# A 5x5 depthwise and grouped convolution in 64x64 quarter products over 6 shifts instead of full 128x128 products over 4

## The chip, the cores and the metric

The kernel runs on one core of a Trainium2 chip. The metric is the device time of one execution, in microseconds (us). The chip's engines work side by side and meet through semaphores: PE (TensorE) multiplies matrices, DVE (VectorE) and ACT (ScalarE) work on vectors and empty PE's accumulator memory (PSUM), POOL (GpSimd) works on vectors in SBUF, SP (SyncE) here only issues DMAs. "PEld" is the load of PE's weights.

## The reference

The input x has 8 images of 256 channels on 64x64 points, in float32. There are two layers, each with a group normalisation ahead of it and a sum with x behind it. Layer 1 is a block-sparse attention that the change does not touch. Layer 0, in its core:

```python
qkv = _conv2d(x, w_qkv)                                    # 256 -> 768 channels, 1x1
agg = _conv2d(qkv, w_dw, groups=3 * td, pad=SCALE // 2)    # 5x5, each channel by itself
agg = _conv2d(agg, w_pw, groups=3 * HEADS)                 # 8 channels -> 8 channels, 1x1
ms = jnp.concatenate([qkv, agg], axis=1)
...
q, k = relu(q), relu(k);  kv = sum over points of k v;  out = q kv / (q sum k)
x = x + _conv2d(out, w_proj)
```

The two convolutions behind qkv are what is changed. 768 channels are 96 groups of 8 channels ("heads" of one of q, k, v), and both convolutions together map the 8 channels of a head to 8 channels through 5x5 taps: tap times mix.

## The kernel before

Each image is worked on alone (the loop over `b`), and layer 0 does it in two passes `g` of 128 channels of each of q, k and v. A pass runs these stages in order:

1. `qkv`: 24 products of the normalised image with the weights (L686), emptied into three padded tiles `RAW[j]` (j for q, k, v) on 128 partitions.
2. sums of k v over the points for the raw half (`kv_sums(0)`, L643 to L655).
3. the convolution, `conv`: 24 pairs of heads.
4. sums for the convolved half (`kv_sums(1)`).
5. attention of the convolved half and the projection (`attend(1, c)`, `project`, L709 and L711), eight chunks of 512 points. In the second pass DVE also takes the statistics of the finished image for layer 1 there (`plane_stats`, L1217).

The 64x64 points are split into 16 planes (every fourth row by every fourth column), each 16x16 with a border of one, so 17x17 = 289 numbers are stored. A head of 8 channels and 16 planes fills the 128 partitions: SP loads it by a DMA from `RAW` into `IN` (L362), and a 5x5 convolution over the points is then four products of 128x128, one for each shift of 0 or 1 in the two directions (L623), over 256 columns. A pair of heads is 8 such products. The weights for them ("toeplitz") are built by POOL, tap times mix, in two operations of 128x512 a pair (L485), from taps that SP loads for eight heads at once (L350). The 2x256 results of a pair lie in one PSUM bank of 512 columns. They are emptied by ACT for even items and by DVE for odd ones (L930 to L932; the helper's lines are L982, L985, L1144 and L1147) into `OUTG`, and two DMAs store them to `AGG` (L374).

PSUM has four banks for this work, used in turn. Each user has an item number `i` and the bank `i % 4`. `claim(i)` on PE waits until the bank's last user has been emptied, `hand(i)` tells the engine that empties it. Before the change a pair is one item. From pair 11 on there is, after every second pair, an `attend(0, c)`: two items, one with the denominators (WD) and one with the numerators (WN), each a product of 512 columns (L666). ACT copies the denominators (L1030), DVE takes their reciprocal (L1234) and multiplies the numerators by it (L1238), which frees their bank. DVE does its share in the order of the program: it empties a pair's bank, then does the division, then the next pair's.

SP issues in program order too: the load for pair k, which waits until PE is through with pair k-3, then the store of pair k-2, which waits until it is emptied. Every DMA here has 128 rows.

X itself stays in natural order in SBUF. The planes are read out of it by strides: with 16 planes a row of 16 numbers has a step of 4 numbers. That is so where layer 0 normalises X into XN (`norm_chunk`, L1010 on ACT and L1207 on DVE), where the projection is added to X (L1247 on DVE, L491 on POOL) and where the statistics are read (L1217).

## Time and profile before

| | |
|---|---|
| median of 3 runs | 9082.88 us (9064.64 to 9105.43) |
| the profiled execution | 9057.69 us, span 9055.9 us |
| PE busy | 7636.7 us, 84% |
| DVE busy | 5037.9 us, 56% |
| POOL, ACT busy | 3786.7 us, 3520.5 us |
| DMA | 431.90 MB in 398743 packets |
| mean granted PE clock | 0.919 of full |
| chain that ended last | PE 54%, DVE 23%, issue 7%, DMA 6% |

A busy share is a mean over stages with different limits. PE is the busiest engine, and the chain that ended last is PE for a little over half of its length; L623, the convolution, is the largest line of it with 12%. In a group of matmuls the mean duration is longer than the pace, since they overlap. One float32 product shows as two matmul records and two weight loads.

### The profile page before, as it was taken

To read this page: it belongs to the slowest core of one execution; us is meant where nothing else is said; L and a number is where in the kernel's file an instruction comes from. 1 tells how busy PE (TensorE), PEld (TensorE's weight loads), DVE (VectorE), ACT (ScalarE), POOL (GpSimd) and SP (SyncE) were. 2 spreads that over 40 slices of the span, in tenths; PEclk is the share of its full clock that TensorE was granted. 3 is DMA by queue.
4 is the path that set the end of the run, shared out by engine and by line. 5 is a ranking of instruction groups with operands and counts; after the bars stand their busy time and mean duration, and the time that the engine had idled before them with its cause. 6 is when DMAs were issued, how large, how long until landed. Compare 5 with 4: busy or idle time off the path is not lost.

```text
span 9055.9 us, 206227 instructions
## 1 busy us (share of the span) xinstructions
PE 7636.7 (84%) x65004; PEld 5190.5 (57%) x65004; DVE 5037.9 (56%) x11563; ACT 3520.5 (39%) x9207; POOL 3786.7 (42%) x10084
## 2 busy tenths in 40 slices
PE   8978799787997879978899778997789977799788
PEld 5655556555565555655555555565555555566555
DVE  3475644756447564475644756447564475644655
ACT  1145621445214552145521455215552155511555
POOL 2345533445334553345533444334443344533444
PEclk9988999888999889988999888998889988999888
DMA  3201122011220112201122111221112211122111
GB/s 101 65 16 26 41 87 65 16 26 38 89 65 16 27 42 85 65 18 26 51 75 65 21 22 49 77 65 21 23 53 73 65 22 22 57 68 65 24 20 55
DMA packets 398743, 431.90 MB, mean 48 GB/s; under 512 B 159184, under 2 KB 355984, under 8 KB 393296
## 3 DMA queue, kind: packets, MB, share of 16 engines
q1 hardware_dynamic: 397648, 418.42, 16.3%
q8 instruction: 550, 9.01, 0.4%
q14 instruction: 545, 4.46, 0.2%
HBM read 102.76 MB, written 67.63 MB: 19 GB/s over the span
## 4 chain that ended last, share of the span: by engine, by line
PE 54%; DVE 23%; issue 7%; DMA 6%; ACT 5%; DVEq 3%; SPq 1%; POOL 0%; ACTq 0%; POOLq 0%
PE PS L623 12%; PE PS L686 7%; DVE arena L1144 5%; PE PS L913 5%; DVE arena L1234 4%; PE PS L778 3%; PE PS L666 3%; PE PS L878 3%; PE PS L838 3%; PE PS L847 3%; DVE SM L1379 3%; ACT arena L1088 3%; DVEq L1367 2%; DMA kv_rows<-arena 2%; PE PS L654 2%
## 5 line engine op out<-in xcount | busy, mean ns | idle before, releaser
L982 ACT ACTIVATE arena<-PS 128x128 f32<-128x128 f32 (+5 forms) x4160 | 1552.0, 399 | 1947.5 <-PE PS L623 596.5
L561 POOL COPY arena<-arena 64x129 f32 x6144 | 1527.9, 291 | 1372.0 <-PE PS L884 1094.0
L485 POOL TENSOR_TENSOR arena<-arena 128x512 f32<-128x512 f32 x768 | 806.2, 1072 | 1459.5 <-PE PS L623 1443.6
L623 PE MATMUL PS<-arena 128*128 128x256 f32 x6144 | 1359.1, 379 | 46.4 <-DMA arena<-arena 46.3
L1144 DVE COPY arena<-PS 64x260 f32<-64x260 f32 (+2 forms) x1272 | 634.3, 515 | 1352.5 <-PE PS L623 524.7
L623 PEld LDWEIGHTS PS<-arena 128*128 128x128 f32 x6144 | 1155.4, 189 | 270.6 <-issue 98.0
L1144 DVE COPY arena<-arena 64x129 f32 x4096 | 840.9, 267 | 398.3 <-PE PS L884 285.9
L1234 DVE RECIPROCAL arena<-arena 128x512 f32<-128x512 f32 x256 | 857.5, 3350 | 119.1 <-ACT arena L1030 117.5
L818 PE MATMUL PS<-arena 64*64 64x192 f32 x8192 | 699.0, 386 | 256.9 <-POOL arena L561 242.0
L491 POOL TENSOR_TENSOR BUF<-BUF,arena 128x512 f32<-128x512 f32 x256 | 358.2, 1399 | 1282.3 <-ACT arena L1018 1282.3
L1379 DVE TENSOR_REDUCE SM<-PS 128x1 f32<-128x384 f32 x1024 | 570.6, 558 | 539.7 <-issue 434.3
L1088 ACT ACTIVATE arena<-PS,SM 128x384 f32<-128x384 f32 x1024 | 595.1, 581 | 638.9 <-DVE SM L1379 598.6
L778 PE MATMUL PS<-W,BUF 128*128 128x192 f32 x4096 | 818.7, 348 | 27.2 <-ACT BUF L1010 20.5
L778 PEld LDWEIGHTS PS<-W,BUF 128*128 128x128 f32 x4096 | 687.2, 197 | 63.2 <-ACT BUF L1010 21.2
L686 PE MATMUL PS<-BUF,W 128*128 128x512 f32 x1536 | 678.8, 604 | 37.5 <-DVE BUF L1207 33.7
L825 PE MATMUL PS<-CST,arena 128*128 128x128 f32 x1024 | 312.1, 337 | 415.9 <-ACT arena L1088 379.7
L838 PE MATMUL PS<-CST,arena 128*128 128x128 f32 x3072 | 589.2, 307 | 52.0 <-ACT arena L1088 51.2
L878 PE MATMUL PS<-arena 128*64 128x65 f32 x12288 | 632.8, 243 | 0.0
L538 POOL TENSOR_TENSOR arena<-arena,SM 128x256 f32<-128x256 f32 x512 | 314.4, 614 | 748.1 <-DVE SM L1322 746.7
L878 PEld LDWEIGHTS PS<-arena 128*64 128x64 f32 x12288 | 483.9, 149 | 196.1 <-issue 193.9
L1147 DVE TENSOR_SCALAR arena<-PS 128x256 f32<-128x256 f32 (+1 forms) x336 | 160.1, 477 | 733.0 <-PE PS L623 432.7
L666 PE MATMUL PS<-arena 128*128 128x512 f32 x1024 | 498.4, 608 | 68.8 <-DVE arena L1241 56.0
(102 smaller groups left out, 10563.4 us busy)
## 6 DMA issues: line engine op xcount, KB each, us to landing
arena<-arena SPq DMA_DIRECT2D x1024, 128.0 KB, 2.3
arena<-arena SPq DMA_DIRECT2D x768, 144.5 KB
BUF<-in_x SPq DMA_DIRECT2D x18, 2048.0 KB, 12.0
kv_rows<-arena SPq DMA_DIRECT2D x256, 130.0 KB, 3.5
arena<-kv_rows SPq DMA_DIRECT2D x256, 130.0 KB
out<-BUF SPq DMA_DIRECT2D x64, 512.0 KB, 2.6
arena<-in_taps SPq DMA_DIRECT2D x96, 288.0 KB, 3.6
W<-in_w SPq DMA_DIRECT2D x2, 768.0 KB, 5.8
```

The costliest lines, as they stand in the source:

```text
L485: last = pool.tensor_tensor(o, tap, mix, ALU.mult)
L561: last = pool.tensor_copy(G[p % GD][0:D, j // 3, j % 3, :], KVB[0:D, bass.ds(off, KVW)])
L623: last = nc.tensor.matmul(bank(i)[:, a * 256:(a + 1) * 256], lhsT=TW[n % 2][:, a * CH + k * P:a * CH + (k + 1) * P], rhs=src[:, k // 2:k / ...
L686: last = nc.tensor.matmul(bank(i), lhsT=W0[:, kt, (2 * j + g) * P:(2 * j + g + 1) * P], rhs=XN[:, kt, c * CH:(c + 1) * CH], start=(kt == 0 ...
L778: last = nc.tensor.matmul(PS[:, p % 2, u * 3 * D:(u + 1) * 3 * D], lhsT=XN[:, kt, t * P:(t + 1) * P], rhs=W1[:, kt, h, :], start=(kt == 0) ...
L838: last = nc.tensor.transpose(PS[:, 4 + p % 2, i * P:(i + 1) * P], PR[p % 2][:, i * P:(i + 1) * P], ident)
L878: nc.tensor.matmul(PS[D * blk:D * (blk + 1), 6 + t % 2, at:at + D1], lhsT=PT[p % 2][:, i * P + D * blk:i * P + D * (blk + 1)], rhs=G[p % G ...
L982: return nc.scalar.activation(o, i, ACT.Copy)
L1088: nc.scalar.activation(PR[p % 2].rearrange("p (i s c) -> p s i c", i=3, s=2), PS[:, 2 * (p % 2):2 * (p % 2) + 2, 0:3 * D].rearrange("p s ( ...
L1144: return nc.vector.tensor_copy(o, i)
L1234: order.after(nc.vector.reciprocal(DN[c % 2], DN[c % 2]))
L1379: nc.vector.tensor_reduce(NM[:, p % 2:p % 2 + 1], PS[:, 2 * (p % 2):2 * (p % 2) + 2, 0:3 * D], AX.XY, ALU.max, negate=True).then_inc(s_nm, 1)
```

## The change

Two by two positions replace the four by four in one direction: the points are now split into 8 planes (every fourth row by every second column), each 16x32 with a border, stored as 17x34 = 578. A head of 8 channels and 8 planes fills 64 partitions, and a pair of heads 128. So a pair is loaded by one DMA from 16 channels that lie on every fourth partition, and stored by one. A 5x5 convolution is now six shifts (two in rows, three in columns) of 64x64 weights. Each product covers 8 rows of 32 points, 256 columns; the two heads and the two halves of the rows make four quarter products for a shift, 24 for a pair. Head `a` sits on partitions 64a to 64a+63 of the input and writes bank `i + a`; half `o` of the rows goes to partitions 64o to 64o+63 of the output. A pair is now two items: ACT empties head 0, DVE head 1, each in two operations of 64x256.

```diff
-PL, R = 16, 16
-PW = R + 1
-PAD = PW * PW
+PL, R, RC2 = 8, 16, 32
+PW, PC = R + 1, RC2 + 2
+PAD = PW * PC
+SHIFTS = 6
-    return g * HALF_ITEMS + (I_CQ + m + 8 if m < 0 else I_CKV + m + 2 * max(0, (m - 2) // 2))
+    return g * HALF_ITEMS + (I_CQ + 2 * (m + 8) if m < 0 else I_CKV + 2 * m + 2 * max(0, (m - 2) // 2))
...
         def natural(tile, fy):
-            return tile.rearrange("p (r fy c fx) -> p fy fx r c", fy=4, c=R, fx=4)[:, fy]
+            return tile.rearrange("p (r fy c fx) -> p fy fx r c", fy=4, c=RC2, fx=2)[:, fy]
...
                         if n >= 3:
                             wait_filled(sp, b, conv_item(n - 3))
+                            settle(sp)
+                            wait_filled(sp, b, conv_item(n - 3) + 1)
...
-                        for a in range(2):
-                            sp.dma_start(IN[n % 3][:, a * PAD:(a + 1) * PAD],
-                                         head_rows(RAW[j], 2 * pr + a).rearrange("p (f n) -> p f n", f=PL)
-                                         ).then_inc(s_in[n % 3], 16)
+                        sp.dma_start(IN[n % 3], pair_rows(RAW[j], pr).rearrange("p (f n) -> p f n", f=PL)
+                                     ).then_inc(s_in[n % 3], 16)
...
-                        for k in range(24 + 2):
+                        for k in range(24 + 3):
                             if k < 24:
                                 load_pair(24 * g + k)
-                            if k >= 2:
-                                store_pair(24 * g + k - 2)
+                            if k >= 3:
+                                store_pair(24 * g + k - 3)
...
-                        for a in range(2):
...
-                            tap = tap.unsqueeze(2).broadcast_to([P, 4, 8, 16])
-                            mix = dw[:, hh, 64:72].unsqueeze(1).unsqueeze(3).broadcast_to([P, 4, 8, 16])
-                            last = pool.tensor_tensor(o, tap, mix, ALU.mult)
-                        last.then_inc(s_tw, 1)
+                        tap = tap.unsqueeze(2).broadcast_to([P, SHIFTS, 8, 8])
+                        mix = dw[:, 8 * SHIFTS:].unsqueeze(1).unsqueeze(3).broadcast_to([P, SHIFTS, 8, 8])
+                        pool.tensor_tensor(o, tap, mix, ALU.mult).then_inc(s_tw, 1)
...
                                 claim(i)
+                                claim(i + 1)
...
-                                for a in range(2):
-                                    src = IN[n % 3][:, a * PAD:(a + 1) * PAD].rearrange("p (r c) -> p r c", r=PW)
-                                    for k in range(4):
+                                for k in range(SHIFTS):
+                                    for a, o in ((0, 0), (1, 1), (0, 1), (1, 0)):
+                                        head = slice(a * D, (a + 1) * D)
+                                        rows = IN[n % 3][head, :].rearrange("p (r c) -> p r c", r=PW)
+                                        y, xx = k // 3 + o * R // 2, k % 3
                                         last = nc.tensor.matmul(
-                                            bank(i)[:, a * 256:(a + 1) * 256],
-                                            lhsT=TW[n % 2][:, a * CH + k * P:a * CH + (k + 1) * P],
-                                            rhs=src[:, k // 2:k // 2 + R, k % 2:k % 2 + R],
-                                            start=(k == 0), stop=(k == 3))
-                                hand(i, last)
+                                            bank(i + a)[o * D:(o + 1) * D, 0:256],
+                                            lhsT=TW[n % 2][head, k * D:(k + 1) * D],
+                                            rhs=rows[:, y:y + R // 2, xx:xx + RC2],
+                                            start=(k == 0), stop=(k == SHIFTS - 1))
+                                        if k == SHIFTS - 1 and o != a:
+                                            hand(i + a, last)
...
-                    if i % 2 == e:
-                        wait_filled(eng, b, i)
-                        eng.wait_ge(s_og[n % 3], b * 512 + 32 * (n // 3 + 1))
-                        op(OUTG[n % 3], PS[:, i % 4, :]).then_inc(s_free[e], 1)
+                    i = conv_item(n) + e
+                    wait_filled(eng, b, i)
+                    eng.wait_ge(s_og[n % 3], b * 256 + 16 * (n // 3 + 1))
+                    op(OUTG[n % 3][e * D:(e + 1) * D, 0:256], PS[0:D, i % 4, 0:256])
+                    op(OUTG[n % 3][e * D:(e + 1) * D, 256:512], PS[D:P, i % 4, 0:256]).then_inc(s_free[e], 1)
```

The taps that the host lays out follow the same split; a load of them is 128x224 numbers instead of 128x576.

Three places show how the change moves the instructions. First PE, at the first of a pass's eight attends and the two pairs behind it: L666 (now L669) is the attend, L623 (now L625) the convolution. Before:

```order
L666 MATMUL PS<-arena 128x512 [waits bank_freed_by_act]
L666 MATMUL PS<-arena 128x512 [waits bank_freed_by_dve]
L605 REGISTER_ALU
L618 REGISTER_ALU [waits bank_freed_by_act]
L619 REGISTER_ALU [waits toeplitz_built]
L623 MATMUL PS<-arena 128x256 [waits conv_in0]
L623 MATMUL PS<-arena 128x256 x7
L618 REGISTER_ALU [waits bank_freed_by_dve]
L623 MATMUL PS<-arena 128x256 [waits conv_in1,toeplitz_built]
L623 MATMUL PS<-arena 128x256 x7
```

And now:

```order
L669 MATMUL PS<-arena 128x512 [waits bank_freed_by_act]
L669 MATMUL PS<-arena 128x512 [waits bank_freed_by_dve]
L603 REGISTER_ALU
L617 REGISTER_ALU [waits bank_freed_by_dve,bank_freed_by_act]
L618 REGISTER_ALU [waits toeplitz_built]
L625 MATMUL PS<-arena 64x256 [waits conv_in0]
L625 MATMUL PS<-arena 64x256 x23
L603 REGISTER_ALU
L617 REGISTER_ALU [waits bank_freed_by_dve,bank_freed_by_act]
L625 MATMUL PS<-arena 64x256 [waits toeplitz_built,conv_in1]
```

A pair waits for two banks, one from each engine, and is 24 products instead of 8. The attend's numerators lie in the bank that the second pair behind it claims.

Next DVE, some rows on in the same stage: the multiplication by the reciprocal, and what follows until the next reciprocal. Before:

```order
L1238 TENSOR_TENSOR arena<-PS,arena 128x2x16x16 [waits item_for_dve,dve_order]
L318 REGISTER_ALU
L931 REGISTER_ALU [waits item_for_dve]
L1144 COPY arena<-PS 128x512 [waits conv_out1]
L1233 REGISTER_ALU
L1234 RECIPROCAL arena<-arena 128x512 [waits bank_freed_by_act]
```

And now:

```order
L1241 TENSOR_TENSOR arena<-PS,arena 128x16x32 [waits item_for_dve]
L317 REGISTER_ALU
L933 REGISTER_ALU [waits item_for_dve]
L1147 COPY arena<-PS 64x256 [waits conv_out0]
L1147 COPY arena<-PS 64x256
L1147 COPY arena<-PS 64x256 [waits conv_out1,item_for_dve]
L1147 COPY arena<-PS 64x256
L1236 REGISTER_ALU
L1237 RECIPROCAL arena<-arena 128x512 [waits bank_freed_by_act]
```

DVE empties half of both pairs between two divisions, where it emptied the whole of one.

Last SP, the loads (L362) and stores (L374) of two pairs. Before:

```order
L362 DMA arena<-arena 128x1x289 [waits item_for_dve]
L362 DMA arena<-arena 128x1x289
L372 REGISTER_ALU
L374 DMA arena<-arena 8x16x256 [waits bank_freed_by_act]
L374 DMA arena<-arena 8x16x256
L318 REGISTER_ALU
L362 DMA arena<-arena 128x1x289 [waits item_for_act]
L362 DMA arena<-arena 128x1x289
```

And now:

```order
L362 DMA arena<-arena 128x1x578 [waits item_for_act,item_for_dve]
L371 REGISTER_ALU
L374 DMA arena<-arena 16x8x512 [waits bank_freed_by_act,bank_freed_by_dve]
L362 DMA arena<-arena 128x1x578 [waits item_for_act,item_for_dve]
L371 REGISTER_ALU
L374 DMA arena<-arena 16x8x512 [waits bank_freed_by_act,bank_freed_by_dve]
```

Four DMAs a pair became two, with twice the bytes each, and the store is that of the pair whose completion the load ahead of it has waited for.

## Rows read from the trace of the kernel before

**Rows 1.** Timeline of PE: the first twelve pairs of one pass, and one attend

```profile
1218.12 14.10 PE L623 MATMUL PS<-arena 128*128 128x256 f32 x64
1233.33 14.07 PE L623 MATMUL PS<-arena 128*128 128x256 f32 x64 [1.11 <-DMA arena<-arena]
1248.29 10.61 PE L623 MATMUL PS<-arena 128*128 128x256 f32 x48 [0.89 <-DMA arena<-arena]
...
1262.62 1.88 PE L666 MATMUL PS<-arena 128*128 128x512 f32 x4
```

**Rows 2.** Timeline of PE: two pairs between attends, and the pass's last pairs

```profile
1297.16 1.88 PE L666 MATMUL PS<-arena 128*128 128x512 f32 x4
1298.88 7.08 PE L623 MATMUL PS<-arena 128*128 128x256 f32 x32
1305.79 1.88 PE L666 MATMUL PS<-arena 128*128 128x512 f32 x4
...
1320.34 0.32 PE L654 MATMUL PS<-CST,arena 128*128 128x128 f32 x1 [2.31 <-DMA arena<-arena]
```

**Rows 3.** Groups by line and shape: busy us, mean ns | idle before, releaser

```profile
L485 POOL TENSOR_TENSOR arena<-arena 128x512 f32<-128x512 f32 x768 | 806.2, 1072 | 1459.5 <-PE PS L623 1443.6 <-DMA arena<-in_taps 15.8
L1144 DVE COPY arena<-PS 64x260 f32<-64x260 f32 x512 | 198.8, 428 | 57.7 <-PE PS L762 50.6
L982 ACT ACTIVATE arena<-PS 64x256 f32<-64x256 f32 x528 | 196.6, 372 | 74.0 <-PE PS L762 65.3 <-PE PS L723 8.6
L1247 DVE TENSOR_TENSOR BUF<-PS,BUF 128x512 f32<-128x512 f32 x128 | 138.9, 1085 | 34.7 <-PE PS L711 34.7
L1217 DVE BATCH_NORM_STATS2 SM<-BUF 128x6 f32<-128x512 f32 x128 | 130.0, 1067 | 0.0
L1241 DVE TENSOR_TENSOR arena<-PS,arena 128x512 f32<-128x512 f32 x128 | 88.5, 692 | 7.2
L1160 DVE BATCH_NORM_STATS2 SM<-BUF 128x6 f32<-128x512 f32 x144 | 88.4, 679 | 2.3 <-DMA BUF<-in_x 2.3
```

**Rows 4.** Source line L818, 64x64 products, one set: ns min/median/max, first and last start

```profile
L818 PE MATMUL PS<-arena x8: 321/334/374, 2915.0 to 2915.2; 64*64 64x192 f32 x8
```

**Rows 5.** Timeline of PE: the same set

```profile
2915.01 0.56 PE L818 MATMUL PS<-arena 64*64 64x192 f32 x8
```

**Rows 6.** Timeline of DVE and of ACT behind the attend at 1297.16

```profile
1298.85 3.35 DVE L1234 RECIPROCAL arena<-arena 128x512 f32<-128x512 f32 x1 [0.71 <-ACT arena L1030]
1302.23 0.69 DVE L1238 TENSOR_TENSOR arena<-PS,arena 128x512 f32<-128x512 f32 x1
...
1298.22 0.60 ACT L1030 ACTIVATE arena<-PS 128x512 f32<-128x512 f32 x1 [3.64 <-PE PS L666]
```

**Rows 7.** Timeline of SP's queue, ahead of the pair at 1248.29

```profile
1243.36 1.37 SPq L362 DMA_DIRECT2D arena<-arena  x2
1244.85 1.35 SPq L374 DMA_DIRECT2D arena<-arena  x2
```

**Rows 8.** Busy us by stretch: PE PEld DVE ACT POOL, PEclk, DMA share, GB/s

```profile
1218.10:1262.60 44.50, 42.32 (x204) 36.17 (x193) 4.10 (x8) 3.59 (x6) 25.68 (x24) 1.00 0.47 146
2885.00:2915.00 30.00, 23.25 (x355) 15.41 (x353) 21.15 (x74) 21.68 (x63) 18.80 (x76) 1.00 0.07 16
1320.30:1331.30 11.00, 9.04 (x125) 6.55 (x126) 6.02 (x8) 2.49 (x8) 0.00 (x0) 0.54 0.01 1
```

**Rows 9.** Timeline of DVE: the end of layer 0 in the second pass

```profile
494.92 0.69 DVE L1241 TENSOR_TENSOR arena<-PS,arena 128x512 f32<-128x512 f32 x1
...
502.40 5.85 DVE L1217 BATCH_NORM_STATS2 SM<-BUF 128x6 f32<-128x512 f32 x6
```

**Rows 10.** Timeline of DVE: L1207 as an image begins, and in layer 1

```profile
1154.28 7.00 DVE L1207 TENSOR_SCALAR BUF<-BUF,SM 128x1024 f32<-128x1024 f32 x4
...
512.00 2.98 DVE L1207 TENSOR_SCALAR BUF<-BUF,SM 128x1024 f32<-128x1024 f32 x4
```

79 lines of the change are left out of this document (40 added, 39 removed).

## The prediction, made before the changed kernel ran

> **What bounds the kernel now.** I read the page first: PE is busy 84% of the span and is 54% of the chain that ended last, so an engine's share alone doesn't say what a stage waits for. The timeline of PE over one convolution does. In its first half PE runs pair after pair without a gap but for two waits of 1.11 and 0.89 us on the load of a pair [rows 1]. 64 passes take 14.10 us there, the last of them 0.38 us long by its record, so the pace is (14.10 - 0.38) / 63 = 0.218 us for 256 columns, and a pair of 16 passes takes 3.46 us. In the second half, pairs and attends follow without any gap: an attend every 1305.79 - 1297.16 = 8.63 us, made of 1.72 for the attend and 6.91 for two pairs [rows 2]. Both halves are bound by PE, and its clock is full in them [rows 8]. The timelines of DVE and ACT say what lies beside it: behind an attend that starts at 1297.16, ACT copies the denominators from 1298.22, DVE's reciprocal runs 3.35 us from 1298.85, and its multiplication ends at 1302.92 [rows 6]. That is 5.76 us after the attend's start, and today nobody waits for it. At the end of the second pass it is DVE that has no gap: from 494.92 to 508.25 it works without a pause, and layer 1 waits for it [rows 9].
>
> **PE's part.** A pair was 8 products, 16 passes; now it is 24 quarter products, 48 passes of 256 columns. What they cost depends on how many quarters run at once, and L818 shows such products: the same four positions in the same order, heads on the halves of the rows, banks apart. A set of eight passes over 192 columns takes 0.56 us, and one pass by itself is recorded with 0.321 [rows 4, 5]. 192 columns at the pace above are 0.163 us, which leaves 0.158 of latency. One after another the set would take 8 x 0.163 + 0.158 = 1.46 us, two at a time 0.81, four at a time 0.48. It takes 0.56, so four run together, with 0.08 for the start. In a long row of such passes the start is paid once, and a round of four costs the columns of one, 0.218 us. 12 rounds: 2.61 us a pair, against 3.46. The weights of 64 columns are loaded beside that, as those of L623 are today. The bounds: 2.61 from below; from above, if each round costs half a set, 0.28 + 0.055 for the 64 more columns, 12 x 0.335 = 4.0 us. I take 2.61, since rows 4 and 5 are one set and its second round starts within 0.24 us of the first.
>
> *First half, twelve pairs.* Today 1262.62 - 1218.12 = 44.5 us [rows 1]. Then 12 x 2.61 = 31.3, if the waits on loads go too. They should: SP spends 1.37 + 1.35 us a pair on issuing four DMAs [rows 7], and with two it spends about 1.4. The load of a pair now waits for nothing but PE's end with the pair three back, so it has two pairs, 5.2 us, to land. The load issued from 1243.36 let PE start at 1248.29, 4.9 us later, with a second issue of 0.68 in between [rows 1, 7]; 4.2 are left. Gain: 13.2 us a pass, and there are 16 passes: 211 us.
>
> *Second half, six cycles from attend to attend.* Here the faster PE meets a wait. The second pair behind an attend claims the bank of its numerators, which DVE frees 5.76 us after the attend began. PE is there after 1.72 + 2.61 = 4.33. So the cycle is 5.76 + about 0.1 for the semaphore + 2.61 = 8.47 us, and against 8.63 only 0.16 x 6 x 16 = 15 us are gained; the other 1.5 us a cycle are idle. DVE's emptying of the first pair comes behind the multiplication and is late for nobody: the next attend claims that bank 2.6 us later. The tail behind pair 23 ends with DVE's divisions and a wait on the stores (2.31 us, [rows 2]), both as now: 0, at most 1 us a pass.
>
> **Emptying.** ACT and DVE each do two operations of 64x256 a pair, by like rows 0.37 and 0.43 us each [rows 3], so up to 0.9 us a pair on each. In the first half 2.61 us a pair cover it; in the second the two sums (0.9 behind the multiplication, 0.9 ahead of the copy of the denominators, where 1.06 are free) stay under cover too. If that cover went, each 0.1 us would cost 0.1 x 96. POOL's weights go from 2 x 1.07 us to one operation of 384 elements, between 0.8 and 1.07 us, hidden either way: 0.
>
> **DMA.** The bytes stay, the packets double in size and halve in number. The engines are busy 0.47 of the first half [rows 8]; by bytes that becomes 0.47 x 3.7 / 2.61 = 0.67, by packets 0.33. I take no wait from it.
>
> **The strides.** Where planes are read out of X the step goes from four numbers to two. That is in no name of the change, but it is in the chain. Over 512 numbers L1247 takes 1085 ns and L1217 1067, with a step of four; L1241 and L1160, the same kinds of operation without a step, take 692 and 679 [rows 3]. A step of two is in no row. It may cost the whole 0.39 us still, or nothing. A price that goes by steps would be near the middle, one that goes by how many numbers lie close together near nothing. I take nothing, since the one measured excess (0.39 of 0.69) is less than a doubling, and two neighbours would share it. The Trainium skill (SBUF — State Buffer, "Door 1: The DMA port swizzle") says that SBUF is read in lines of 16 bytes and that two hits on a line are enough for full speed. By that, four numbers' step has one hit a line and pays, two has two and is free; the sum would be the same as mine, and no run here shows it yet. In the second pass DVE does 8 of L1247 and 16 of L1217 in one unbroken row [rows 9]: 24 x 0.38 = 9.1 us an image, a few tenths less where PE is the limit in the first chunks; 8 x 8.8 = 70 us. In the first pass PE sets the pace there: 0. As an image begins, PE waits for the first of four L1207, which take 7.00 us instead of layer 1's 2.98 [rows 10]; a quarter of the difference, 1.0 us, 8 times: 8 us.
>
> **Sum.** 211 + 15 + 70 + 8 = 304 us off 9057.69: 8754 for an execution like the profiled one. That one is 25 us under the median of the runs shown, which gives a predicted median of 8778 us.
>
> **Rivals.**
> - *The strides give nothing.* For it: no row has a step of two. Against it: the thought above. The time: 8778 + 78 = 8856. Chance 0.17.
> - *The rounds don't chain.* Each shift's four quarters wait for the four before, for weights or for the sums in PSUM, and a pair costs between 3.0 and 4.0 us. For it: rows 4 and 5 show two rounds, not twelve. At 3.4: the first half gains 44.5 - 40.8 = 3.7 x 16 = 59, the cycle is 5.86 + 3.4 = 9.26 and loses 0.63 x 96 = 60, the strides stay: 9005. At 4.0 it is 9178, slower. Chance 0.09. The Trainium skill (TensorE: Matmul & The Clock Gate, "Part 3: Packing small matmuls — row/col tiling") gives 3.07 for four tiles where the ideal is four; on this kernel's 48 passes of 0.218 that would be 3.41 us a pair, near this case's 3.4, and the trace has 0.56 for a set where one after another would be 1.46.
> - *Only two quarters run at once*, in two halves of the array. A pair is 24 x 0.218 = 5.23 us: the first half 62.8, 18.3 more; the cycle 1.72 + 10.46 = 12.2, 3.55 more, six times; 16 x (18.3 + 21.3) = 634 more, minus 78: 9639 us, slower. It decides from 3.6 us a pair on, where gain and loss meet. Against it: the set's 0.56 is under the 0.81 of two at a time. Chance 0.05.
> - *A wait takes PE's place in the first half*: loads that land later at 0.67 of the DMA engines, so that a pair takes 3.1 us and not 2.61. It costs 0.49 x 12 x 16 = 94 us: 8872; where the later loads reach the second half too, 8915. Chance 0.06.
> - *The clock falls in the new gaps.* PE idles 1.5 us of every 8.5. In the attention of layer 1, where PE is busy 23.25 of 30 us, the clock stayed full; behind the wait of 2.31 us it fell, and the stretch from 1320.3 on had 0.54 [rows 8]. Each cycle in which the second pair runs at 1.2 GHz costs 2.61 us; a third of them 84 us: 8862. Chance 0.04.
>
> **Chances and range.** The forecast has 0.59. The range: down to 8690, if the tail and the emptying give something back and the start of an image gains more; up to 8910, which takes in the strides, the waits and the clock. What can be told from no change is 0.5%, 45 us. Faster: 0.59 + 0.17 + 0.06 + 0.04 and half of the unchained case, 0.91. Within 0.5%: 0.02. Slower: 0.07.
>
> **What would show it.** In the profile of the changed kernel: passes of L625 with a busy time of 2.6 us a pair; twelve pairs in 31 to 32 us without a wait on a DMA; attends 8.4 to 8.5 us apart with an idle time of 1.5 us that DVE's multiplication ends; the operations on X at 0.69 us instead of 1.08; SP's queue with 1.4 us a pair. I am wrong if a pair's passes take over 3 us, if the attends move apart, or if L1217's successor still takes over 0.9 us.

## The result, and the profile after

The changed kernel took 8942.72 us (median of 4 runs, 8914.77 to 8950.0) against 9076.4 us before in the same session (4 runs): a ratio of 0.984, 95% interval 0.981 to 0.9875. It is faster by 134 us where 304 were forecast, and the median lies above the upper end of the range, 8910 us.

The profiled execution of after has a span of 8935.5 us, 120 us less than before. The starts of the same instructions in the two traces split it up (all 8 images, 16 passes; "first half" from the first pair of a pass to its first attend, "second half" the six cycles from attend to attend):

| part | forecast | measured |
|---|---|---|
| first half, 45.04 to 35.02 us a pass | -211 | -160 |
| second half, 52.02 to 54.60 us a pass | -15 | +41 |
| tail of the convolution, two kinds of pass | 0 | +6 |
| second pass, attention to statistics, 57.77 to 51.39 us | -70 | -51 |
| start of an image, 16.49 to 15.75 us | -8 | -6 |
| layer 1, 640.7 to 646.6 us an image | 0 | +47 |
| sum | -304 | -123 (spans: -120) |

The 3 us between the two sums are in stages that the change does not touch. The 6 us at the start of an image are within scatter: seven such starts last from 13.4 to 18.3 us in after, and in the second trace of the same kernel their mean is 16.4. Now the views. Pairs are counted from 0. First PE's timeline over the same pass as [rows 1] (start, us, engine, line, operation, count, and in brackets the idle time ahead and what ended it):

```profile
1208.10 10.59 PE L625 MATMUL PS<-arena 64*64 64x256 f32 x192
1218.86 2.82 PE L625 MATMUL PS<-arena 64*64 64x256 f32 x48 [0.17 <-issue]
1222.77 8.00 PE L625 MATMUL PS<-arena 64*64 64x256 f32 x144 [1.08 <-issue]
1231.65 5.72 PE L625 MATMUL PS<-arena 64*64 64x256 f32 x96 [0.88 <-issue]
1237.67 5.56 PE L625 MATMUL PS<-arena 64*64 64x256 f32 x96 [0.30 <-issue]
1243.16 1.99 PE L669 MATMUL PS<-arena 128*128 128x512 f32 x4
1245.08 2.82 PE L625 MATMUL PS<-arena 64*64 64x256 f32 x48
1249.47 2.82 PE L625 MATMUL PS<-arena 64*64 64x256 f32 x48 [1.57 <-DVE arena L1241]
1252.23 1.99 PE L669 MATMUL PS<-arena 128*128 128x512 f32 x4
```

Four pairs in a row, 192 passes, take 10.59 us, one pair by itself 2.82; so three pairs add 7.77, 2.59 us each. That is the forecast's 2.61: the rounds of four chain. But the first half has four breaks, where the kernel before had the two of [rows 1] and one of 0.19 us, and between two attends there is a wait on DVE's L1241. Attends are 1252.23 - 1243.16 = 9.07 us apart, where [rows 2] had 8.63. The page calls the breaks "issue". In the trace every one of the 77 breaks over 0.15 us in the 16 first halves ends 0.09 to 0.14 us behind the last landing of the load for the pair that then starts, and together they make 3.5 us a pass. They are not all at pairs 4 and 8: most of the time goes at pairs 6 (0.9 us a pass in the mean), 4 (0.7) and 8 (0.5), and the other pairs from 5 on have 0.2 to 0.4 each.

SP's queue over the first breaks (L362 load, L374 store, L349 the taps), and POOL's building of the weights of pair 3:

```profile
1211.02 0.54 SPq L362 DMA_DIRECT2D arena<-arena  x1
1211.99 0.56 SPq L374 DMA_DIRECT2D arena<-arena  x1
1214.57 0.33 SPq L349 DMA_DIRECT2D arena<-in_taps  x1
1215.09 0.54 SPq L362 DMA_DIRECT2D arena<-arena  x1
1215.81 0.57 SPq L374 DMA_DIRECT2D arena<-arena  x1
1216.50 0.69 SPq L362 DMA_DIRECT2D arena<-arena  x1
...
1213.69 0.85 POOL L484 TENSOR_TENSOR arena<-arena 128x384 f32<-128x384 f32 x1 [1.74 <-PE PS L625]
```

An issue costs 0.55 us at the least and 0.68 in the mean of the first halves, 1.4 us a pair for the 2.7 of [rows 7]. The load of pair 4 could have gone when PE was through with pair 1, at 1213.51. It went at 1215.09, behind the taps, which waited until POOL had built the weights of pair 3, at 1214.54. Four transfers then leave within 2.6 us, and the load issued at 1216.50 lands at 1222.68, 6.2 us later; PE starts its pair at 1222.77.

DVE and ACT around the attend at 1243.16:

```profile
1243.32 0.86 DVE L1147 COPY arena<-PS 64x256 f32<-64x256 f32 x2 [1.88 <-PE PS L625]
1244.96 3.35 DVE L1237 RECIPROCAL arena<-arena 128x512 f32<-128x512 f32 x1 [0.78 <-ACT arena L1033]
1248.44 0.69 DVE L1241 TENSOR_TENSOR arena<-PS,arena 128x512 f32<-128x512 f32 x1
...
1244.33 0.60 ACT L1033 ACTIVATE arena<-PS 128x512 f32<-128x512 f32 x1 [0.28 <-PE PS L669]
```

The chain is that of [rows 6], each link a little later: the denominators 1.17 us behind the attend's start (1.06), the division 1.80 (1.69), the multiplication's end 5.97 (5.76). Then 0.34 us to the pair's start (forecast 0.1) and 2.76 from there to the next attend (forecast 2.61).

The windows of this pass's two halves (length, busy us of PE, PEld, DVE, ACT and POOL, clock, DMA share, GB/s), against [rows 8]:

```profile
1208.10:1243.20 35.10, 32.58 (x577) 25.14 (x577) 9.89 (x25) 8.35 (x22) 12.31 (x13) 1.00 0.79 172
1243.20:1297.80 54.60, 44.89 (x603) 26.61 (x600) 34.45 (x36) 12.70 (x30) 18.11 (x17) 1.00 0.52 127
```

The clock stays full through the gaps. The DMA engines' share rose from 0.47 to 0.79, not to 0.67 (0.79 is also its mean over all 16 first halves). And the groups that answer to [rows 3] (busy us, mean ns, idle before):

```profile
L625 PE MATMUL PS<-arena 64*64 64x256 f32 x18432 | 1063.4, 378 | 196.3 <-DVE arena L1241 154.5 <-issue 25.2 <-DMA arena<-arena 14.3
L1250 DVE TENSOR_TENSOR BUF<-PS,BUF 128x512 f32<-128x512 f32 x128 | 87.7, 685 | 59.0 <-PE PS L714 57.9
L1220 DVE BATCH_NORM_STATS2 SM<-BUF 128x6 f32<-128x512 f32 x128 | 81.0, 679 | 0.0
L484 POOL TENSOR_TENSOR arena<-arena 128x384 f32<-128x384 f32 x384 | 331.8, 866 | 1782.9 <-PE PS L625 1775.7
```

L1250 and L1220 are the old L1247 and L1217: 685 and 679 ns for 1085 and 1067. L1241's 154.5 us of idle time in front of L625 are 1.6 us in each of 96 cycles.

### The profile page after: what moved, and what is told of

It reads as the page before. It is cut to its first block, busy times and chain, and to the rows that moved or that the text cites. A ratio compares the mean times of both kernels' runs of the same rounds, so it can differ in the third digit from the quotient of the medians.

```text
span 8935.5 us, 233739 instructions
## 1 busy us (share of the span) xinstructions
PE 7402.7 (83%) x77292; PEld 4819.9 (54%) x77292; DVE 5140.2 (58%) x12139; ACT 3664.1 (41%) x9783; POOL 3287.1 (37%) x9700
## 4 chain that ended last, share of the span: by engine, by line
PE 51%; DVE 26%; issue 8%; ACT 6%; DMA 5%; DVEq 3%; POOL 1%; SPq 0%; POOLq 0%; ACTq 0%
PE PS L625 8%; PE PS L689 8%; DVE arena L1237 8%; DVE arena L1147 5%; PE PS L916 5%; PE PS L781 3%; PE PS L881 3%; PE PS L841 3%; PE PS L850 3%; DVE SM L1382 3%; DMA kv_rows<-arena 3%; PE PS L669 3%; ACT arena L1091 2%; DVEq L1370 2%; PE PS L657 2%
## 5 line engine op out<-in xcount | busy, mean ns | idle before, releaser
L985 ACT ACTIVATE arena<-PS 128x128 f32<-128x128 f32 (+4 forms) x4544 | 1667.7, 390 | 2185.4 <-PE PS L625 782.5
L1147 DVE COPY arena<-PS 64x256 f32<-64x256 f32 (+5 forms) x1656 | 762.8, 473 | 1209.9 <-PE PS L689 528.0
L625 PE MATMUL PS<-arena 64*64 64x256 f32 x18432 | 1063.4, 378 | 196.3 <-DVE arena L1241 154.5
L625 PEld LDWEIGHTS PS<-arena 64*64 64x64 f32 x18432 | 767.1, 133 | 516.4 <-issue 348.6
L484 POOL TENSOR_TENSOR arena<-arena 128x384 f32<-128x384 f32 x384 | 331.8, 866 | 1782.9 <-PE PS L625 1775.7
L821 PE MATMUL PS<-arena 64*64 64x192 f32 x8192 | 720.7, 393 | 244.7 <-POOL arena L559 227.2
L489 POOL TENSOR_TENSOR BUF<-BUF,arena 128x512 f32<-128x512 f32 x256 | 327.1, 1278 | 1296.7 <-ACT arena L1021 1296.7
L689 PE MATMUL PS<-BUF,W 128*128 128x512 f32 x1536 | 678.5, 604 | 31.3 <-DVE BUF L1210 23.0
L828 PE MATMUL PS<-CST,arena 128*128 128x128 f32 x1024 | 321.5, 347 | 433.2 <-ACT arena L1091 399.0
L841 PE MATMUL PS<-CST,arena 128*128 128x128 f32 x3072 | 605.3, 313 | 55.8 <-ACT arena L1091 54.8
L985 ACT ACTIVATE arena<-arena 64x129 f32 x2048 | 519.8, 300 | 93.5 <-POOL arena L522 48.8
L1150 DVE TENSOR_SCALAR arena<-PS 64x256 f32<-64x256 f32 (+1 forms) x528 | 224.2, 425 | 574.0 <-PE PS L658 303.5
```

Of the source, the lines that this page charges most:

```text
L625: last = nc.tensor.matmul(bank(i + a)[o * D:(o + 1) * D, 0:256], lhsT=TW[n % 2][head, k * D:(k + 1) * D], rhs=rows[:, y:y + R // 2, xx:xx ...
L689: last = nc.tensor.matmul(bank(i), lhsT=W0[:, kt, (2 * j + g) * P:(2 * j + g + 1) * P], rhs=XN[:, kt, c * CH:(c + 1) * CH], start=(kt == 0 ...
L821: last = nc.tensor.matmul(PS[D * blk:D * (blk + 1), 2 * (p % 2) + side, 0:3 * D], lhsT=(lower, upper)[side][:, cols], rhs=G[p % GD][rows, ...
L841: last = nc.tensor.transpose(PS[:, 4 + p % 2, i * P:(i + 1) * P], PR[p % 2][:, i * P:(i + 1) * P], ident)
L985: return nc.scalar.activation(o, i, ACT.Copy)
L1147: return nc.vector.tensor_copy(o, i)
```

## The experiments

All ratios are to the kernel before, timed in the same job; the intervals are of 95%. The theory at the start: the second half is set by DVE's hold on the numerators' bank; the first half by the loads; the operations on X run at the pace that was forecast for a step of two.

**The kernel after, once more** (no edit), the yardstick of its job.

> The changed kernel once more, beside the experiments of the same chip. Layer 1, which no edit touches, took 47 us more in its first profile than in that of the kernel before (32 attention stretches of 91 to 102 us, in both). If that is the phase of the clock and not the change, its 8 stretches from one statistics operation to the next come out anywhere within some 30 us of the 5126 of before, on either side, and the ratio to before stays at 0.98. If the change does slow layer 1, they stay at 5170 or more in this run and in all the others.

8936.34 us, ratio 0.9862 (0.9822 to 0.9902). First half 34.90, cycle 9.10, layer 1 646.2 us an image: each part comes back as it was.

**Four input buffers.** `IN` and its semaphores from three to four:

```
-        IN = [l0.take(PAD) for _ in range(3)]
+        IN = [l0.take(PAD) for _ in range(4)]
...
-                        if n >= 3:
-                            wait_filled(sp, b, conv_item(n - 3))
+                        if n >= 4:
+                            wait_filled(sp, b, conv_item(n - 4))
...
```

> Four input buffers instead of three, so a load starts a pair earlier. Theory A: in the first half of the convolution PE waits because a load now lands 5.5 us after its issue, later than the 5.2 us that two pairs take; then the twelve pairs go from 35.0 us (mean of 16 passes, start of the first to the first attend) to 31.5 to 32, and the kernel gets 50 us faster than the changed one (some 8890). Rival B: the DMA engines themselves are the limit (busy 0.79 there), so an earlier issue only makes each load take longer: the twelve pairs stay at 34 or more, gain under 15 us. Rival C: it is the weights of POOL or the emptying: no change at all.

8928.52 us, 0.9846 (0.9805 to 0.9887); first half 35.07, unchanged. The loads may start a pair earlier, but in the trace those of pairs 4 to 11 leave only 0.43 us earlier in the mean: they still stand behind the taps and the stores in SP's queue. And they take 0.48 us longer to land (5.90 for 5.42). A deeper buffer alone buys nothing.

**Numerators in banks of their own.** The raw half's numerators go to two PSUM banks outside the four, and the second pair behind an attend no longer waits for DVE's multiplication (its `claim` is changed to the bank's user before that, in lines that are not shown):

```
...
-                                hand(i, nc.tensor.matmul(bank(i), lhsT=w, rhs=q, start=True, stop=True))
+                                o = PS[:, (4, 7)[c % 2], :] if src == 0 and w is WN[0] else bank(i)
+                                hand(i, nc.tensor.matmul(o, lhsT=w, rhs=q, start=True, stop=True))
```

> The numerators of the raw half's attends go to the two PSUM banks that layer 0 leaves idle then, and the second pair behind an attend no longer waits for DVE's division. Theory A: the cycle from attend to attend (9.06 us now, 8.63 before the change) is set by that wait; it falls to what PE needs, 1.92 + 2.6 + 2.6 = 7.1 to 7.3 us, 16 x 6 x 1.8 = 175 us less: near 8770. Rival B: with the wait gone the loads are late here too, as in the first half: 7.8 to 8.3 us a cycle, 70 to 120 us less. Rival C: DVE itself is the limit, with 3.35 + 0.69 + 4 x 0.43 and its gaps, 6.0 us: then nothing below 7.1 can be seen and A holds.

8752.03 us, 0.9654 (0.9618 to 0.9689). PE's timeline:

```profile
1222.51 1.98 PE L675 MATMUL PS<-arena 128*128 128x512 f32 x4
1224.43 5.41 PE L630 MATMUL PS<-arena 64*64 64x256 f32 x96
1229.77 1.99 PE L675 MATMUL PS<-arena 128*128 128x512 f32 x4
```

No gap is left, the cycle from attend to attend is 7.26 us, and in the six cycles PE is busy throughout:

```profile
1222.51:1266.07 43.56, 43.56 (x605) 24.99 (x601) 34.45 (x36) 12.72 (x30) 18.15 (x17) 1.00 0.62 153
```

(9.10 - 7.26) x 96 = 177 us was the price of that wait. The cycle is made of 1.92 from attend to pair, 5.34 from there to the next attend: two pairs at 2.59 would be 5.18, and an attend took 1.72 between full products [rows 2]. So each cycle pays 0.2 us behind the attend and 0.16 ahead of it, where TensorE goes from whole-array products to quarters and back. The Trainium skill (TensorEngine Tiling (Array Packing), "Key Properties") says that a change of the tiling mode drains the engine. The trace fits that, with 0.36 us for two changes; no run here tells a drain from another cause.

**Without the division.** DVE's reciprocal of the raw half over one column instead of 512, so this run leaves out that division:

```
-                            order.after(nc.vector.reciprocal(DN[c % 2], DN[c % 2]))
+                            width = 1 if src == 0 else CH
+                            dn = DN[c % 2][:, 0:width]
+                            order.after(nc.vector.reciprocal(dn, dn))
```

> Leaves the reciprocal of the raw half's denominators out, but for one column. DVE frees the numerators' bank about 3.2 us earlier, 2.8 us behind the attend's start, before PE has ended the first pair at 4.5. Theory A: the same cycle as with other banks, 7.1 to 7.3 us, and beside it the end of a pass's raw attends gets shorter by the two divisions, 3 to 6 us a pass. So the kernel gains 175 + 50 to 100 us against the changed one: 8670 to 8720. Rival B (the wait isn't DVE's but that of the loads or of POOL): the cycle stays above 8 us.

8658.03 us, 0.9555 (0.9507 to 0.9602). The cycle is 7.26 again, the same by another road: bank or division, one link of one chain. The other 94 us against the banks are the tail of the convolution, from a pass's seventh attend to the convolved half's first: 20.1 us and not 26.0, since DVE's last divisions end the pass.

**The kernel before, once more** (no edit, one execution, so no ratio).

> The kernel before, unchanged, profiled once more. In the trace of before layer 1 of the eight images takes 5126 us (from the layer's statistics to the next ones), in the four traces of kernels with the change's layout 5169 to 5185. If that is an effect of the change (where its tensors lie or how the pace of the attention falls in), this trace has again 5120 to 5135; if the first profile was a lucky execution, 5150 to 5190. Layer 0's pieces are to come out as before: conv's first half 45.0 us a pass, six cycles of the second half 52.0 us.

9075.43 us. First half 45.26, cycle 8.65; layer 1 5142 us.

**Each load in two transfers of half the columns.**

```
+                        for a in range(2):
+                            part = slice(a * PAD // 2, (a + 1) * PAD // 2)
+                            sp.dma_start(IN[n % 3][:, part],
+                                         pair_rows(RAW[j], pr).rearrange("p (f n) -> p f n", f=PL)[:, :, part]
+                                         ).then_inc(s_in[n % 3], 16)
...
```

> The kernel after with each pair's load as two transfers of 289 columns, so packets of 1156 B instead of 2312 B; the same bytes and source partitions. Theory A, the size of the packets makes them slow (2312 B took 168 ns in the median, 1156 B 52 ns in the kernel before, so 1.6 times as much a byte): packets of 52 to 70 ns, landings 1 us earlier, the 3.2 us of waits on loads go from the 35.0 us of the first half (to 31.8 to 32.5), 16 passes: 40 to 50 us less than the kernel after, ratio to the kernel before 0.980. Rival B, the bytes in flight at once (loads and stores together at 172 GB/s) are the limit: packets take their share whatever their size, 75 to 85 ns for a half, first half 34.5 to 35.5, time within 10 us of the kernel after, 0.985. Rival C, SP's issues (two of 0.55 us and one of 0.56 us a pair, 1.7 of 2.6 us, and waits between them) become the limit: 3.1 us a pair, slower by 60 us, 0.992.

8921.25 us, 0.985 (0.9827 to 0.9873). The window of one first half:

```profile
1206.84:1241.34 34.50, 31.87 (x577) 25.68 (x577) 9.84 (x25) 8.37 (x22) 12.33 (x13) 1.00 0.63 169
```

The packets did get cheaper: 53 ns in the median for 1156 B (68 in the mean), where 2312 B had taken 168 (166), and the DMA share falls from 0.79 to 0.63 in this window, to 0.67 over all first halves. The first half's mean is 33.8 us, 1.2 less, between what theory A and rival B expected. The trace says why it isn't more. A load of pairs 4 to 11 has now landed 4.39 us behind its first issue, where it took 5.42. But it leaves 1.08 us behind the moment when its buffer is free, where it left after 0.65: SP issues three DMAs a pair and needs longer to catch up behind the taps. So the landing did get shorter by 1.0 us, and SP's queue took 0.4 of it back.

**Each load in two transfers of one head.** Packets of 2312 B as in after, each transfer to 64 partitions:

```
+                        for a in range(2):
+                            first = 64 * (pr // 4) + pr % 4 + 32 * a
+                            rows = RAW[j][first:first + 29:4, :].rearrange("p (f n) -> p f n", f=PL)
+                            sp.dma_start(IN[n % 3][a * D:(a + 1) * D, :], rows).then_inc(s_in[n % 3], 16)
...
```

> The kernel after with each pair's load as two transfers of one head each: packets stay 2312 B, each transfer reads 8 partitions instead of 16 and writes 64. It has the issues of the split by columns without its small packets. Theory A (size of the packets): packets stay at 150 to 170 ns, first half 35 us or a little more, time within 15 us of the kernel after. Rival B (limit by bytes): the same. Rival D, the many partitions that one transfer touches, or the queue that handles one transfer at a time, make it slow: two transfers in a row overlap less with one another, first half changes by over 1 us in either direction, time by over 15 us. With the split by columns faster and this one not, the size of the packets is shown.

8974.01 us, 0.9916 (0.9891 to 0.9941): slower than after, first half 37.2 us.

```profile
1221.44:1259.22 37.78, 33.09 (x576) 25.00 (x576) 9.80 (x24) 8.35 (x22) 12.29 (x13) 1.00 0.62 158
```

The share is again 0.62, but with less moved. With the same number of issues as the split by columns it is 3.4 us a pass worse. The packets of 2312 B take 122 ns in the median here (134 in the mean), not the 150 to 170 that theory A expected, so a packet's size alone doesn't set its time. Yet a pair's load needs 6.15 us from its first issue to its last landing. Which property of the transfer does that isn't shown. In the trace the semaphore of such a transfer is raised in 9 steps, that of a transfer to 128 partitions in 16, so fewer engines may share it. The Trainium skill (SBUF — State Buffer, "Door 1: The DMA port swizzle") has the 64 lower partitions reach only half of the ports; that would fit, but no view here shows ports.

**Banks, and loads and stores split.** The bank edit above, the split by columns, and the store split in the same way.

> The kernel after with three edits: the raw half's numerators in PSUM banks of their own (as in the banks experiment, 8752 us), each pair's load in two transfers of 1156 B packets and each pair's store in two of 1024 B packets. Theory A (size of the packets): the first half's waits go too, 3.2 us x 16 = 50 us less than 8752, so 8700, ratio 0.960. Rival B (limit by bytes): 8745 to 8760, 0.9655. Rival C (SP's four issues a pair, 2.2 us of 2.6): the pairs are paced by SP at 3 to 3.4 us, 8800 to 8850, 0.973.

8763.98 us, 0.9675 (0.9655 to 0.9695); first half 35.8 us, no better than after's 35.0. This doesn't refute that smaller packets help, since another limit took over. The loads have landed 3.88 us behind their first issue, sooner than in any other run, but they leave 2.43 us behind the moment when the buffer is free: SP's issues fill 27.7 us of the 35.8. That is rival C, the queue, though the time is less than the 8800 to 8850 it expected.

**The taps one pair later.** This changes the order of SP's queue:

```
-                        if n % 4 == 0 and 1 <= n // 4 <= 10:
+                        if n % 4 == 1 and 1 <= n // 4 <= 10:
```

> The kernel after with the load of the next taps issued ahead of the load of pairs 5, 9, 13, ... instead of 4, 8, 12, ... In the trace of the kernel after SP issued the taps at 1214.57, when GpSimd had built the weights of pair 3, and behind them within 2.5 us load 4, store 1 and load 5; load 4 could have gone at 1213.1, when pair 1 had freed its buffer. Theory E, the in-order queue: loads 4 and 8 go 1.5 us earlier and the transfers no longer come in a bunch, landings of loads 4, 5, 8 and 9 come before their pair, and the first half falls from 35.0 us to 32.5 to 33.5 a pass; 16 passes: 25 to 40 us less than the kernel after, ratio to the kernel before 0.982. Rival B, the transfers' volume is the limit: the wait only moves to other pairs, first half 34.5 to 35.2, time within 10 us of the kernel after. Rival F: the later taps are late for GpSimd's weights, pairs 5 and 9 wait on them, first half over 36, slower.

8910.92 us, 0.9827 (0.98 to 0.9855). PE's timeline of the pass:

```profile
1209.70 13.19 PE L625 MATMUL PS<-arena 64*64 64x256 f32 x240
1223.59 10.59 PE L625 MATMUL PS<-arena 64*64 64x256 f32 x192 [0.71 <-issue]
1234.46 2.82 PE L625 MATMUL PS<-arena 64*64 64x256 f32 x48 [0.27 <-DMA arena<-arena]
1237.70 5.44 PE L625 MATMUL PS<-arena 64*64 64x256 f32 x96 [0.42 <-issue]
```

SP's queue says why (the load of pair 4 is the third row):

```profile
1212.62 0.54 SPq L362 DMA_DIRECT2D arena<-arena  x1
1213.59 1.03 SPq L374 DMA_DIRECT2D arena<-arena  x1
1215.21 0.54 SPq L362 DMA_DIRECT2D arena<-arena  x1
1216.08 0.57 SPq L374 DMA_DIRECT2D arena<-arena  x1
1216.77 0.70 SPq L349 DMA_DIRECT2D arena<-in_taps  x1
1217.81 0.76 SPq L362 DMA_DIRECT2D arena<-arena  x1
```

Load 4 goes 5.5 us behind the pass's start, no longer 7.0, and pair 4 starts without a break. The waits that go there come back in part at pairs 5 and 9: the first half is 33.97 us, 1.05 less, and not the 1.5 to 2.5 expected. All loads now leave within 0.3 us of the moment when their buffer is free (in the mean of each pair), but they still take 5.58 us to land, and 2.5 us of breaks a pass remain. (The expectation's 1213.1 for pair 1's end is the start of its last product; the end is 1213.51.)

**Banks and later taps.** Both edits.

> The raw half's numerators in banks of their own (8752 us alone) and the taps' load one pair later. Theory E: the two are in different halves of a pass, so their gains add: 8752 less 25 to 40 is 8712 to 8727, ratio 0.962. Rival B: 8745 to 8760, 0.9655.

8743.82 us, 0.9645 (0.962 to 0.967). First half 34.44 against 34.62 with the banks alone: 3 us in 16 passes. Here the expectation of 25 to 40 us fails: by the first halves the later taps are worth 17 us in the kernel after and 3 us beside the banks, where the loads take 5.72 us to land. Why they land later there isn't shown.

**The same with four buffers for input and output.** The edits of four input buffers, and `OUTG` to four as well.

> As the last, and four buffers instead of three for the pairs' input and for their output. With the taps no longer ahead of load 4 the fourth buffer lets a load go 2.6 us earlier. Theory E with room left on the DMA engines: all waits on loads go, first half 31.5 to 32.3 us, time 8695 to 8710, ratio 0.960. Rival B, volume is the limit: landings take longer by what they start earlier, as in the run with four input buffers alone; time within 10 us of the run before this one.

8710.72 us, 0.9606 (0.9581 to 0.9631). PE's timeline:

```profile
1191.25 24.13 PE L630 MATMUL PS<-arena 64*64 64x256 f32 x432 [0.23 <-issue]
1216.51 8.00 PE L630 MATMUL PS<-arena 64*64 64x256 f32 x144 [1.13 <-issue]
```

First half 32.62 us. The fourth buffer, worth nothing while the taps stood in front of load 4, is now worth 1.8 us a pass: the loads leave 0.9 us earlier than without it, and take the same 5.7 us to land. The output's fourth buffer wasn't tried by itself, but the trace shows no part of it in the first half: a pair's emptying ends 0.94 to 1.04 us behind its last product with three as with four. So it is two things together: the queue must let the load go, and a buffer must be free for it.

**A step of four put back.** x is read by planes at a step of 4, in an order that is not the reference's:

```
-            return natural(X[:, kt, :], c // 2)[:, c % 2]
+            return X[:, kt, :].rearrange("p (r q c fx) -> p q fx r c", q=2, c=RC2, fx=4)[:, c // 4, c % 4]
```

> The kernel after with layer 0's x read and written by planes at a step of 4 fp32 in place of 2 (L1250's add, L1220's statistics and GpSimd's adds at L489), in an order that isn't the reference's, so this run leaves out which channel meets which; sizes and counts are as they were. It puts a step of 4 back where the change brought a step of 2. Theory A, the step sets their pace: the add of 512 columns takes 1085 ns again instead of 685, the statistics 1067 instead of 679, and the stretch from the second half's first raw chunk to the statistics 57.8 us instead of 51.4: 8 x 6.4 = 51 us more than the kernel after, 8987, ratio 0.9915. Rival: another part of the change (what stores or loads run beside them) made them faster: 685 and 679 ns stay and the time is that of the kernel after.

8983.08 us, 0.991 (0.9886 to 0.9934), and the groups:

```profile
L1250 DVE TENSOR_TENSOR BUF<-PS,BUF 128x512 f32<-128x512 f32 x128 | 138.7, 1083 | 34.9 <-PE PS L714 34.9
L1220 DVE BATCH_NORM_STATS2 SM<-BUF 128x6 f32<-128x512 f32 x128 | 130.0, 1070 | 0.0
```

The stretch is 58.0 us and the time 4 us from the expected 8987. The step sets the pace of these operations: nothing else was put back. The rule of the Trainium skill that was weighed ahead (SBUF — State Buffer, "Door 1: The DMA port swizzle", two hits on a line of 16 bytes) holds: the trace agrees, with 685 ns at two hits and 1083 at one.

**The order of the quarters.** The loops of a pair exchanged, the same 24 products:

```
-                                for k in range(SHIFTS):
-                                    for a, o in ((0, 0), (1, 1), (0, 1), (1, 0)):
+                                for a, o in ((0, 0), (1, 1), (0, 1), (1, 0)):
+                                    for k in range(SHIFTS):
```

> The kernel after with the two inner loops of a pair exchanged: all six shifts of one quarter in a row, then the next quarter, the same 24 products. Theory A, products overlap only with the neighbours in the program that are on other quarters: at most two quarters meet at the three borders, a pair takes 20 to 24 x 0.43 = 8.6 to 10.4 us instead of 2.6, 384 pairs: 2300 to 3000 us more, 11300 to 11900. Rival, TensorE looks ahead over several products and fills the quarters however they are ordered: 2.6 to 4 us a pair, under 9400.

10539.42 us, 1.1632 (1.1607 to 1.1656). The group of the quarter products:

```profile
L625 PE MATMUL PS<-arena 64*64 64x256 f32 x18432 | 2854.4, 379 | 1.7 <-issue 0.8
```

A pair takes 7.14 us for 2.59: 2854.4 us busy, not 1063.4. That is less than the 8.6 to 10.4 expected. The starts show why: in a row of one quarter five passes come 216 ns apart, while around a border they come in twos, 55 and 160 ns apart. So the overlap reaches some passes past the border, not one; but six shifts in a row are beyond it. The order of the loops is worth a factor of 2.75 on the same products.

**The kernel before without the division.** The edit of the run without the division, on the kernel before; this run leaves out the same division.

> The kernel before, with the raw half's reciprocal over one column instead of 512, so this run leaves out the division of the raw numerators. Theory A (in the kernel before TensorE's work of two pairs and an attend, 8.67 us, sets the second half's cycle, DVE has slack): the cycle stays at 8.6 to 8.7 us, and only the end of a pass, where DVE's divisions follow one another, is shorter by 6 us: 16 x 6 = 96 us less, 8960. Rival: DVE already set a part of the cycle and it falls under 8.5 us. On layer 1: if any shorter layer 0 costs it clock, layer 1 takes 5165 to 5190 us and the time is 8995; if it is the change itself, 5120 to 5150.

8992.6 us, 0.9925 (0.9904 to 0.9947). Its attends stay 8.645 us apart (8.670 in before):

```profile
1291.64 1.88 PE L666 MATMUL PS<-arena 128*128 128x512 f32 x4
1293.36 7.08 PE L623 MATMUL PS<-arena 128*128 128x256 f32 x32
1300.27 1.88 PE L666 MATMUL PS<-arena 128*128 128x512 f32 x4
```

In the old kernel the division was free in the cycle; in the new one it costs 1.84 us of each. Only the tail is shorter, by 5.0 us a pass.

**All edits, and loads split by columns.**

> As the run with banks, later taps and four buffers (8711 us), and each pair's load in two transfers of 289 columns (1156 B packets). Theory A (packets of 2312 B take 168 ns where two of 1156 B take 104): the 1.4 us a pass that is left of the waits on loads goes, 8680 to 8700. Rival (the queue of issues on SP, now three a pair, and the bytes are what is left): first half 32.6 us or more, 8705 to 8730.

8685.84 us (8684.5 to 8703.95), ratio 0.9589 (0.9567 to 0.9611), the fastest kernel that leaves nothing out. A pass's twelve pairs run as one row:

```profile
1182.60 31.59 PE L633 MATMUL PS<-arena 64*64 64x256 f32 x576 [0.23 <-issue]
```

First half 31.86 us in the mean, 0.76 less than without the split, 12 us in all. The medians differ by 25 us, but the intervals overlap, and in the two profiled executions layer 1, which no edit touches, differs by 17 us; so the other 13 us are not shown to be a gain.

## Why the prediction was wrong

The direction held, and so did the pair: 2.59 us measured, 2.61 forecast, and the order experiment shows what that rests on. The two rivals on the array, no chaining (3.4 us a pair) and two quarters at a time (5.23), are both far from it. The strides: a step of two is free, as taken (685 and 679 ns), shown by the step put back. Of their 78 us the last stage gave 51 and not 70, since some of DVE's saved time turns into waits on PE (L1247's idle time in [rows 3] was 34.7 us, its successor L1250 has 59.0); the 6 us at the start of an image are within scatter. The 8 forecast there were too many: they put the whole of 7.00 - 2.98 us down to the step. In the first image L1207 took 1.20 us at a step of four and its successor L1210 0.81 at a step of two, as in layer 1 without one; in the later images both have about 0.6 us more, whose cause isn't shown. SP's issue times came as forecast (1.4 us a pair). The emptying (376 and 423 ns) and POOL's weights (866 ns) stayed hidden.

**The step that failed in the first half** is "it has two pairs, 5.2 us, to land ... 4.2 are left", and with it "the load of a pair now waits for nothing but PE's end with the pair three back". The table has the loads of pairs 4 to 11 in the 16 first halves, from the starts and landings in the traces. "Leaves" is the first issue behind PE's end with the pair that frees the buffer when there are three of them, "lands" the last landing behind that first issue:

| run | leaves | lands | sum | first half |
|---|---|---|---|---|
| before (a pair 3.46 us) | 2.44 | 5.17 | 7.61 | 45.04 |
| by head | 0.81 | 6.15 | 6.96 | 37.22 |
| banks, loads and stores split | 2.43 | 3.88 | 6.31 | 35.79 |
| four input buffers | 0.22 | 5.90 | 6.12 | 35.07 |
| after | 0.65 | 5.42 | 6.07 | 35.02 |
| banks and later taps | 0.17 | 5.72 | 5.89 | 34.44 |
| later taps | 0.16 | 5.58 | 5.74 | 33.97 |
| split by columns | 1.08 | 4.39 | 5.47 | 33.80 |
| banks, later taps, four buffers | -0.71 | 5.70 | 4.99 | 32.62 |
| all these, and split by columns | -0.34 | 4.80 | 4.46 | 31.86 |

With quarter products the first half falls as the sum falls, from run to run; a mean under 5.2 still leaves single loads above it. The larger error is the landing: 5.42 us, not 4.2. The 4.2 came from one load of before with its second issue taken off; the mean of all of them there is 5.17, or 4.5 by the same reckoning. The smaller error is the 0.65 in SP's queue, 1.6 and 1.7 us for pairs 4 and 8 behind the taps, which wait for POOL, which waits for PE. Moving the taps took away nearly all of that and gave back 1.05 of the 3.5 us of breaks; the rest needed the fourth buffer and the split. A first half of 35.02 us for the forecast's 31.3 makes 60 us in 16 passes; the gain fell short by 51, since the sum started from one pass of 44.5 us where the mean before was 45.04.

The two breaks of [rows 1] lie four pairs apart, as the taps do, and the prediction put them down to SP's issue time. In the trace of before both had a part. The store ahead of the taps had gone out at 1227.51, and the weights of pair 3 were ready at 1227.46:

```profile
1226.16 1.35 SPq L374 DMA_DIRECT2D arena<-arena  x2
1227.64 0.40 SPq L350 DMA_DIRECT2D arena<-in_taps  x1
1228.08 1.34 SPq L362 DMA_DIRECT2D arena<-arena  x2
...
1225.39 2.07 POOL L485 TENSOR_TENSOR arena<-arena 128x512 f32<-128x512 f32 x2 [1.39 <-PE PS L623]
```

With the issues halved only POOL's wait was left there, and it was in no term.

The rival with later loads came closest, with 3.1 us a pair (measured mean 2.92) and loads that land later; it had a chance of 0.06. Its reason, the DMA engines' share, is shown in part: with the same bytes in two transfers the share fell from 0.79 to 0.67 and the landing by 1.0 us. Whether it is the packets' size, the transfer's or the share that counts isn't told apart. What gave back 3.2 us together was the queue's order, a fourth buffer and the split (35.0 to 31.9).

**The step that failed in the second half** is the cycle of 5.76 + 0.1 + 2.61 = 8.47. The mechanism was right and named, and both runs that take the hold away show it: DVE's hold on the bank takes PE's place. But a hold is a chain, and each of its links was mis-sized in one direction: 5.97 for 5.76, 0.34 for 0.1, 2.76 for 2.61. Together that is 0.6 us, a cycle of 9.07 in this place and of 9.10 in the mean, more than the old 8.67 that PE alone had set. A gain of 15 us became a loss of 41. A part of the 0.6 is the change between whole-array and quarter products: the attend itself is recorded with 1.99 us for 1.88, and 0.16 stands ahead of the next one, as with banks of their own. The rest is in small gaps, such as 0.13 us for 0.03 between DVE's division and its multiplication; that is read from the trace, and wasn't tried by itself.

**What was in no term** is layer 1, +47 us in the first pair of traces. Its code is the same. The sums of the eight layer 1 windows (length, then busy us), before and after:

```profile
sum 5125.92, PE 4091.39 PEld 2935.10 DVE 3166.67 ACT 2780.87 POOL 2535.46; mean PE 511.42 PEld 366.89 DVE 395.83 ACT 347.61 POOL 316.93
```

```profile
sum 5172.89, PE 4122.97 PEld 2958.69 DVE 3186.30 ACT 2776.45 POOL 2537.64; mean PE 515.37 PEld 369.84 DVE 398.29 ACT 347.06 POOL 317.21
```

ACT and POOL do not change, PE's busy time rises by 32 us and DVE's by 20, and an image is long where PE's granted clock is low. Two windows of after:

```profile
4926.49:5587.19 660.70, 534.25 (x5518) 382.59 (x5518) 405.50 (x1201) 346.94 (x977) 316.75 (x1101) 0.82 0.13 31
...
7165.05:7804.64 639.59, 504.32 (x5518) 362.56 (x5518) 396.14 (x1200) 346.87 (x977) 317.08 (x1101) 0.89 0.13 32
```

Added up, PE's clock was at 1.2 GHz for 1289 us of layer 1 in before and 1401 in after; the difference at half speed is 56 us of PE's pace. The three traces with before's convolution have 5126, 5142 and 5131 us. Of the fourteen with quarter products twelve have 5168 to 5190, and two have 5145 (the order of the quarters) and 5151 (all edits). Within one job the old convolution stands at 5142 against 5177 to 5190, and in another at 5131 against those two. Against a shorter layer 0 as the reason speaks one trace: 5131 is that of the kernel before without the division. How a layer of the same code comes to less clock behind the quarter products stays open; it is 14 to 48 us, of the 181 by which the forecast was off.

## What to carry to other kernels

When one engine gets faster inside a cycle, work out the whole chain of the engine that comes next, with a semaphore gap at each link; here the slack was forecast as 0.16 us of 8.63 and the links grew by 0.6, so the cycle ended longer than it was. A free PSUM bank turned +41 us into -135. For a load, add up both parts, how long it waits in the queue and how long it takes to land, and take them from many loads and not from one. Read waits by their period: what comes every four pairs stands in an in-order queue ahead of everyone. And try remedies in pairs, since a deeper buffer by itself showed no effect while the queue's order was still in front of it.

## What the runs showed of the hardware

- Quarter products of 64x64 at float32 on four positions chain without loss: 48 passes of 256 columns add 2.59 us, 54 ns each. In another order of the same products it is 149 ns.
- Going from whole-array products to quarter products and back costs about 0.36 us for both changes (1.92 us for 1.72 behind the attend, 5.34 for 5.18 ahead of the next).
- DMA packets from SBUF to SBUF, with other transfers beside them: 2312 B took 168 ns in the median (166 in the mean) when one transfer filled 128 partitions, and 122 (134) when each transfer filled 64; 1156 B took 53 (68). So the same size had different times, and a packet's size is only a part of it.
- A load of 289 KB within SBUF landed 5.4 us behind its issue with the DMA engines busy 0.79, and 4.4 us behind the first issue when it was split by columns (0.67).
- On DVE a step of two float32 in SBUF costs nothing in an addition and in the statistics (685 and 679 ns for 512 numbers), a step of four 1083 and 1070. On GpSimd an addition of 512 took 1278 ns at a step of two and 1399 at four.
